# Two transformer layers on one core: where tiles are turned, and in what order each engine works

## The chip, the core and the metric

One core of a Trainium2 chip runs the kernel. The metric is the device time of one execution in microseconds (us), the median over three runs. A profiled execution gives a trace besides; its times are those of the hardware profiler.

## What is computed

The input x has 16 batches of 256 tokens with 512 features, the context 16 x 256 x 384. Two layers follow each other, each an attention to the context and a feed-forward part, cut here to what matters:

```
x = x + L0_xattn(layernorm(x), ctx)     # 16 heads of 32; Q and K normalised to length 1; layer norm with gamma, beta behind
x = x + L0_ffn(layernorm(x))            # times a 512 x 512 Hadamard matrix, rounded to 4 bits, times ternary weights
x = x + L1_xattn(layernorm(x), ctx)     # 16 heads of 32, scores clipped at 1e4
x = x + L1_ffn(layernorm(x))            # 512 -> 2048 -> 512, ternary W1 and W2, exact gelu
```

A matrix product contracts over the partitions, so its left operand has to stand turned, features on partitions. Every fp32 operand is split into an upper fp16 half and a lower one (what is left), and three fp16 products stand for one fp32 product.

## The kernel before

The program is written engine by engine, with semaphores; no scheduler moves anything. It has two phases.

**Phase A** takes the three first sums batch by batch. Its work is cut into steps ("tasks"), in four streams: 0f (front of layer 0: load, layer norm, turn x and ctx, project q, k, v), 0b (heads of layer 0, output projection, and the Hadamard feed-forward), 1f (front of layer 1, with the maxima of the scores) and 1b (heads of layer 1 and its output projection). In iteration i the streams work on batches i, i-1, i-2 and i-3, so there are 19 iterations: 3 in which the streams start, 13 steady ones (3 to 15) and 3 in which they run out. A fifth stream "w" prepares weights in the first two and the last three. A string of digits (`ORDER`, and `ORDERS` for the special iterations) says from which stream the next task comes. All five engines go through this same sequence, each doing its own part of a task.

A **head** task does several things for different heads: ACT takes exp of head h (L946, PSUM to fp32) and casts head h-1 to the upper fp16 half (L954), GpSimd (POOL in the trace) subtracts to get the lower half of h-1 (L802), TensorE multiplies head h-4 with the values (L1510 to L1512), DVE divides a finished group of four (L1246, L1249). In layer 1 DVE clips the scores first (L1166) and TensorE then adds the shift of the softmax (L1413). Scores of a quad of heads are 24 matmuls (L1488).

**Turning.** Where a tile has to stand turned, TensorE transposes 128 x 128 blocks in fp32 into a bank of PSUM (L1352, `turn`), ACT copies the bank to the upper half (L884, `hi`) and DVE subtracts to the lower half (L1084, `lo`). That is done for ctx (6 blocks a batch), x of layer 0 (8), x of layer 1 (8), the attention output of layer 0 (8) and 1 (8), and the input of the Hadamard product (8). Already turned by DMA from fp16 rows are q and k of layer 0 (L678) and the rounded levels (L682): SP issues transposing DMAs.

```
def turn(u, src, chunks, after=()):
    open_bank(u, *after)
    for c in range(chunks):
        mm = te.transpose(bank(u.bank)[:, c * P:(c + 1) * P], src[:, c * P:(c + 1) * P], ident)
    mm.then_inc(filled[u.bank], 1)
```

SP's queue issues all loads and stores but that of x1: it loads x (L647) for the next batch behind the store of x2 (L701), and works in the order of the tasks too. DVE takes the statistics of x (L1073, L1075), GpSimd four small operations for the reciprocal deviation (L769 to L775), and ACT normalises (L879).

W1 and W2 of the last feed-forward part are made ternary at the end of phase A: ACT sums their absolute values (L864), DVE makes the signs (L1063, L1068), TensorE turns them (L1313, 128 transposes) and ACT copies them out of PSUM (L872, L875).

**Phase B** is that last part, in 8 steps of two batches with 16 blocks each: TensorE multiplies up (L1530, `up`), ACT applies gelu (L1002), DVE casts (L1276), GpSimd or DVE subtracts (L834, L1281), TensorE multiplies down (L1540, `down`). The normalised x of the next step (L1078, written by `norm_b` at blocks 7 to 10) is turned by TensorE in the same way, at blocks 9 to 12 (L1523), with ACT (L995) and DVE (L1269) behind; it is needed by the `up` that runs in block 14.

## Time and profile before

| | |
|---|---|
| median of 3 runs | 1884.29 us (1883.42 to 1885.39) |
| the profiled execution | 1877.33 us, span of its trace 1875.5 us |
| TensorE (PE) busy | 1673.7 us, 89% of the span |
| DVE busy | 1225.7 us, 65% |
| ACT busy | 1027.6 us, 55% |
| GpSimd (POOL) busy | 980.5 us, 52% |
| granted clock of TensorE, mean | 0.961 of full speed |
| DMA | 136.47 MB, 73 GB/s in the mean |

A row of the trace has the engine, the line of the code, the operation, the tile written and the tiles read. A wait is booked to the engine that waited, with what released it. A matmul's own duration is longer than the time that it adds in a row of matmuls, since they are pipelined; the distance of starts tells that.

### The profile page before, as it was taken

To read this page: it belongs to the slowest core of one execution; us is meant where nothing else is said; L and a number is where in the kernel's file an instruction comes from. 1 tells how busy PE (TensorE), PEld (TensorE's weight loads), DVE (VectorE), ACT (ScalarE), POOL (GpSimd) and SP (SyncE) were. 2 spreads that over 40 slices of the span, in tenths; PEclk is the share of its full clock that TensorE was granted. 3 is DMA by queue.
4 is the path that set the end of the run, shared out by engine and by line. 5 is a ranking of instruction groups with operands and counts; after the bars stand their busy time and mean duration, and the time that the engine had idled before them with its cause. 6 is when DMAs were issued, how large, how long until landed. Compare 5 with 4: busy or idle time off the path is not lost. (4 is left out here: it accounts for less than half of the span.)

```text
span 1875.5 us, 44682 instructions
## 1 busy us (share of the span) xinstructions
PE 1673.7 (89%) x18098; PEld 986.8 (53%) x18098; DVE 1225.7 (65%) x2444; ACT 1027.6 (55%) x1905; POOL 980.5 (52%) x1073
## 2 busy tenths in 40 slices
PE   5688898998989999989998999977759999999999
PEld 2445655556555565555565555554534444444444
DVE  4748778787787867878687786857854433344332
ACT  4663867758677586765758667586542222222221
POOL 1553857648576485855758567483353222322221
PEclk9789999999999999999999999988968999999999
DMA  7322231322313123031330313236320110011100
GB/s 225 93 88 59 65 111 24 111 58 66 111 24 111 33 91 111 19 110 25 106 100 24 111 24 111 62 112 206 112 68 19 45 45 12 34 45 46 45 23 23
DMA packets 132379, 136.47 MB, mean 73 GB/s; under 512 B 91464, under 2 KB 95688, under 8 KB 131152
## 3 DMA queue, kind: packets, MB, share of 16 engines
q1 hardware_dynamic: 129872, 125.23, 22.6%
q0 software_dynamic: 2304, 8.39, 1.1%
q8 instruction: 145, 2.38, 0.5%
q14 instruction: 58, 0.48, 0.1%
HBM read 72.77 MB, written 31.46 MB: 56 GB/s over the span
## 5 line engine op out<-in xcount | busy, mean ns | idle before, releaser
L802 POOL TENSOR_TENSOR arena<-arena 128x512 f16<-128x512 f32 x512 | 598.6, 1194 | 123.8 <-ACT arena L954 123.1
L946 ACT ACTIVATE arena<-psum 128x512 f32<-128x512 f32 x512 | 311.0, 614 | 78.2 <-PE psum L1413 68.1
L954 ACT ACTIVATE arena<-arena 128x512 f16<-128x512 f32 x512 | 330.5, 653 | 7.6 <-PE psum L1512 7.3
L1002 ACT ACTIVATE arena<-psum,arena 128x512 f32<-128x512 f32 x128 | 88.1, 688 | 352.1 <-PE psum L1530 352.1
L1332 PE MATMUL psum<-arena 128*128 128x512 f16 x672 | 259.8, 387 | 3.5 <-DVE arena L1084 1.8
L1333 PE MATMUL psum<-arena 128*128 128x512 f16 x672 | 258.4, 385 | 0.0
L1336 PE MATMUL psum<-arena 128*128 128x512 f16 x672 | 257.8, 384 | 0.0
L1510 PE MATMUL psum<-arena 128*128 128x33 f16 x2048 | 199.3, 180 | 62.2 <-POOL arena L802 57.3
L834 POOL TENSOR_TENSOR arena<-arena 128x512 f16<-128x512 f32 x64 | 77.3, 1208 | 333.9 <-DVE arena L1276 333.9
L1530 PE MATMUL psum<-arena 128*128 128x512 f16 x1024 | 243.1, 381 | 1.4 <-DVE arena L1269 1.4
L1540 PE MATMUL psum<-arena 128*128 128x512 f16 x1016 | 240.0, 379 | 0.9 <-POOL arena L834 0.9
L1276 DVE CAST arena<-arena 128x512 f16<-128x512 f32 x128 | 54.6, 427 | 272.1 <-ACT arena L1002 272.1
L1510 PEld LDWEIGHTS psum<-arena 128*128 128x128 f16 x2048 | 167.8, 97 | 116.7 <-POOL arena L802 54.1
L814 POOL TENSOR_TENSOR arena<-arena 128x512 f32<-128x512 f32 x32 | 40.0, 1269 | 311.4 <-DVE arena L1220 311.4
L1512 PE MATMUL psum<-arena 128*128 128x33 f16 x2048 | 195.9, 178 | 0.0
L1511 PE MATMUL psum<-arena 128*128 128x32 f16 x2048 | 195.8, 178 | 0.0
L1488 PE MATMUL psum<-arena 32*128 32x256 f16 x4608 | 166.0, 276 | 14.1 <-DVE arena L1128 5.1
L1166 DVE TENSOR_SCALAR psum<-psum 128x512 f32<-128x512 f32 x256 | 158.9, 690 | 29.1 <-PE psum L1488 29.1
L1511 PEld LDWEIGHTS psum<-arena 128*128 128x128 f16 x2048 | 165.3, 97 | 16.3 <-issue 0.3
L1530 PEld LDWEIGHTS psum<-arena 128*128 128x128 f16 x1024 | 100.4, 98 | 123.5 <-issue 1.9
L1512 PEld LDWEIGHTS psum<-arena 128*128 128x128 f16 x2048 | 163.6, 96 | 0.0
L1540 PEld LDWEIGHTS psum<-arena 128*128 128x128 f16 x1016 | 99.2, 98 | 115.0 <-POOL arena L834 1.9
(129 smaller groups left out, 3155.9 us busy)
## 6 DMA issues: line engine op xcount, KB each, us to landing
arena<-in_x SPq DMA_DIRECT2D x32, 512.0 KB, 4.7
arena<-x_scratch SPq DMA_DIRECT2D x32, 512.0 KB, 5.2
arena<-in_L_ffn_W SPq DMA_DIRECT2D x16, 1024.0 KB, 5.4
arena<-arena SPq DMA_DIRECT2D x16, 512.0 KB, 6.5
x_scratch<-arena POOLq DMA_DIRECT2D x16, 512.0 KB, 5.7
x_scratch<-arena SPq DMA_DIRECT2D x16, 512.0 KB, 3.0
out<-arena SPq DMA_DIRECT2D x14, 512.0 KB, 3.5
arena<-in_ctx SPq DMA_DIRECT2D x16, 384.0 KB, 5.2
```

The costliest lines, as they stand in the source:

```text
L802: gp.tensor_tensor(pl[l][:, h % NP, :], pf[l][:, h % NF, :], ph[l][:, h % NP, :], ALU.subtract).then_inc(p_lo[l].sem, 1)
L946: sc.activation(pf[l][:, h % NF, :], bank(u.bank), ACT.Exp, scale=SCALE / (QS * QS) if l == 0 else SCALE).then_inc(read[u.bank], 1)
L954: sc.activation(ph[l][:, h % NP, :], pf[l][:, h % NF, :], ACT.Copy).then_inc(p_hi[l].sem, 1)
L1332: te.matmul(out, x_hi, w[:, 0, c, :], start=(c == 0), stop=False)
L1333: te.matmul(out, x_hi, w[:, 1, c, :], start=False, stop=False)
L1336: mm = te.matmul(out, x_lo, w[:, 0, c, :], start=False, stop=(c == chunks - 1))
L1488: mm = te.matmul(bank(u.bank)[:, k * S:(k + 1) * S], parts[own][rows_g, j, m, k * P:(k + 1) * P], parts[other][rows_g, 1 - j, m, :], start ...
L1510: te.matmul(out, p_hi_t, vs[l][:, k, h, 0:OW], start=(k == 0), stop=False)
L1511: te.matmul(out[:, 0:HD], p_hi_t, vs[l][:, k, h, HD + 2:VP], start=False, stop=False)
L1512: mm = te.matmul(out, p_lo_t, vs[l][:, k, h, 0:OW], start=False, stop=(k == NT - 1))
L1530: mm = te.matmul(bank(4 + f % 2), w1T[:, c, f * P:(f + 1) * P], xTb[slot][:, part, c, :], start=(c + part == 0), stop=(c + part == DC))
L1540: mm = te.matmul(bank(k), src[:, f % NG, k * P:(k + 1) * P], w2T[:, f, :], start=(f + n == 0), stop=(f + n == FC))
```

## The change

1. **Turned by DMA.** For layer 0's x, both attention outputs and the Hadamard input the tile is no longer transposed by TensorE. ACT copies the rows to an fp16 upper half, DVE subtracts to the lower half (both inputs now in SBUF), both halves stand side by side in one row of 1024, and a transposing DMA on SP puts them where the products read them (`turn_rows`). Layer 1's x is still turned by TensorE. The same is done for the normalised x in phase B (`upper_b`, `lower_b`, `turn_b`).
2. **ctx, W1 and W2** are handed over turned. One ACT copy and one DVE subtraction of 128 x 768 per batch make the halves of ctx; the signs of W1 and W2 are written where they are used.
3. **Orders.** `ORDER` and `ORDERS` give every engine its own sequence of the same tasks. TensorE's sequence decides which bank a task gets.
4. In phase B's first step the statistics of x no longer stand behind the last output of phase A.

The core of the diff:

```diff
+def turn_rows(dst, rows, k):
+    return sp.dma_start_transpose(dst.rearrange("p s c n -> p (s c) n")[:, :, k * P:(k + 1) * P],
+                                  rows[:, k].rearrange("p s n -> p (s n)"))
...
 # SP
+elif kind == "split_x" and l == 0:
+    sp.wait_ge(xT_lo.sem, xT_lo.at(b, k + 1))
+    if b > 2:
+        sp.wait_ge(qk_hi.sem, qk_hi.at(b - 3))
+    turn_rows(xT[0], x_rows, k).then_inc(xT_turned[k].sem, 16)
+elif kind == "split_out":
+    sp.wait_ge(oT_lo[l].sem, oT_lo[l].at(b, k + 1))
+    if l == 1 and b + 2 < B:
+        sp.wait_ge(absmax.sem, absmax.at(b + 2, k + 1))
+    turn_rows(oT[l], out_rows[l], k).then_inc(oT_turned[l][k].sem, 16)
+elif kind == "split_ffn":
+    sp.wait_ge(xF_lo.sem, xF_lo.at(b, k + 1))
+    turn_rows(oT[0], out_rows[0], k).then_inc(xF_turned[k].sem, 16)
...
 # ACT
 elif kind == "turn_out":
-    hi(use["ot", l, at[0]], cols(oT[l], 0, at[0]), oT_hi[l].sem)
+    last = use["o", l, H // HG - 1]
+    act.wait_ge(read[last.bank], last.read_at)
+    sc.activation(out_rows[l][:, k, 0, :], attn[l][:, k, :], ACT.Copy).then_inc(oT_hi[l].sem, 1)
...
 # DVE
 elif kind == "split_out":
-    lo(use["ot", l, k], cols(oT[l], 1, k), cols(oT[l], 0, k), oT_hi[l].sem, oT_hi[l].at(b, k + 1))
+    dve.wait_ge(oT_hi[l].sem, oT_hi[l].at(b, k + 1))
+    v.tensor_tensor(out_rows[l][:, k, 1, :], attn[l][:, k, :], out_rows[l][:, k, 0, :],
+                    ALU.subtract).then_inc(oT_lo[l].sem, 1)
 elif kind == "split_ctx":
-    lo(use["c", 0, k], cols(cT[0], 1, k), cols(cT[0], 0, k), ctxT_hi.sem, ctxT_hi.at(b, k + 1))
+    dve.wait_ge(ctxT_hi.sem, ctxT_hi.at(b))
+    v.tensor_tensor(cT[0][:, 1], CT, cT[0][:, 0], ALU.subtract).then_inc(ctxT_lo.sem, 1)
...
 # TensorE
-elif kind == "turn_out":
-    turn(use["ot", l, k], attn[l][:, k, :], DC, [use["o", l, g] for g in range(H // HG)] if k == 0 else [])
 elif kind == "out_project":
-    open_bank(u, use["ot", l, k])
+    open_bank(u)
+    pe.wait_ge(oT_turned[l][k].sem, oT_turned[l][k].at(b))
...
 # orders: one of the tables
+    "steady": {
+        "SP": ("0210000000011111111111111111111111111111100000000031111111111110000000003333333333333333333333333333"
...
 # phase B, TensorE
-        if has_next and 0 <= f - TURN_AT < BT:
-            turn_b(s + 1, f - TURN_AT)
...
-                pe.wait_ge(xTb_read, s * BT + 2 * BT)
+                pe.wait_ge(xTb_turned, 16 * BT * (s + 2))
...
 # host
+arrays["in_ctx_768"] = np.ascontiguousarray(inputs["ctx_768"].transpose(0, 2, 1))
+for name in ("L1_ffn_W1", "L1_ffn_W2"):
+    arrays[f"in_{name}"] = np.ascontiguousarray(inputs[name].T)
```

How the orders move the work, at three places of a steady iteration. First TensorE where an iteration begins: x8 is the ternary product of the batch before, x48 two quads of scores of layer 0. Before:

```order
L1456 MATMUL psum<-arena 128x512 x8
L1405 MATMUL psum<-arena 128x128 x2
L1488 MATMUL psum<-arena 128x256 x48
L1342 MATMUL psum<-arena 128x256
L1344 MATMUL psum<-arena 128x256
L1345 MATMUL psum<-arena 128x256
```

and with the change (L1557 is the old L1456, L1509 the old L1405, L1587 the old L1488, L1609 to L1611 the old L1510 to L1512):

```order
L1557 MATMUL psum<-arena 128x512 x8
L1509 MATMUL psum<-arena 128x128 x2
L1587 MATMUL psum<-arena 128x256 x48
L1609 MATMUL psum<-arena 128x33
L1610 MATMUL psum<-arena 128x32
L1611 MATMUL psum<-arena 128x33
```

Behind the scores stood the projection of layer 1's keys (L1342 to L1346, 40 narrow matmuls); now the first heads' products with the values stand there.

Second DVE at the same point: the last output of layer 1 (L1182, now L1298), maxima (L1154, now L1268), the shifts (L1160, now L1274), the ternary output (L1220, now L1338), then the statistics of the next x. Before:

```order
L1182 SCALAR_TENSOR_TENSOR arena<-psum,arena 128x512
L1154 TENSOR_REDUCE arena<-psum 128x2 x4
L1160 TENSOR_SCALAR arena<-arena 128x2x2x4
L1128 SCALAR_TENSOR_TENSOR arena<-psum,arena 128x16x32
L1220 SCALAR_TENSOR_TENSOR arena<-psum,arena 128x512 x2
L1073 BN_STATS arena<-arena 128x6
```

and with the change:

```order
L1268 TENSOR_REDUCE arena<-psum 128x2 x6
L1298 SCALAR_TENSOR_TENSOR arena<-psum,arena 128x512
L1274 TENSOR_SCALAR arena<-arena 128x2x2x4
L1338 SCALAR_TENSOR_TENSOR arena<-psum,arena 128x512 x2
L1179 BN_STATS arena<-arena 128x6
L1181 BN_AGGR arena<-arena 128x2
```

Four maxima and the values' lower half (L1128) no longer stand between the last output and the statistics.

Third SP over one iteration, from the store of x2 on (L701, now L808; the load of x is L647, now L736). Before:

```order
L701 DMA x_scratch<-arena 128x1024
L653 DMA arena<-ctx_scratch 128x768
L647 DMA arena<-in_x 128x2x512
L648 DMA arena<-in_ctx 128x2x384
L633 DMA arena<-in_x 128x2x512
L635 DMA arena<-arena 128x1024
L640 DMA arena<-x_scratch 128x1024
L685 DMA ctx_scratch<-arena 128x768
L678 DMA_TRANSPOSE arena<-arena 128x8x128 x4
L682 DMA_TRANSPOSE arena<-arena 128x4x128 x2
```

and with the change:

```order
L808 DMA x_scratch<-arena 128x1024
L736 DMA arena<-in_x 128x2x512
L737 DMA arena<-in_ctx 128x3x256
L742 DMA arena<-ctx_scratch 128x768
L722 DMA arena<-in_x 128x2x512
L724 DMA arena<-arena 128x1024
L790 DMA ctx_scratch<-arena 128x768
L713 DMA_TRANSPOSE arena<-arena 128x8x128 x4
L767 DMA_TRANSPOSE arena<-arena 128x8x128 x2
L729 DMA arena<-x_scratch 128x1024
L713 DMA_TRANSPOSE arena<-arena 128x8x128 x2
L767 DMA_TRANSPOSE arena<-arena 128x8x128 x2
L713 DMA_TRANSPOSE arena<-arena 128x8x128 x2
L787 DMA_TRANSPOSE arena<-arena 128x4x128 x2
```

Eight transposing DMAs are added (L713 of the change); those of q and k (L678, now L767) stand between them.

## Rows read from the trace of the kernel before

**Rows 1.** Windows of the steady part, the drain and phase B: busy us and count of each engine, clock, DMA share.
```profile
174.00:1214.00 1040.00, 952.95 (x12868) 606.41 (x12870) 807.23 (x1681) 708.94 (x1383) 677.56 (x754) 0.99 0.26 73
1214.00:1412.00 198.00, 139.22 (x1949) 94.50 (x1942) 139.06 (x236) 120.01 (x202) 107.36 (x97) 0.81 0.38 128
1412.00:1875.50 463.50, 456.92 (x2163) 213.67 (x2162) 171.68 (x338) 104.01 (x159) 120.16 (x107) 0.99 0.09 32
```

**Rows 2.** Timeline of SP: a store of x2, the load of x behind it, the last store.
```profile
415.04 0.32 SPq L701 DMA_DIRECT2D x_scratch<-arena  x1
...
415.88 0.78 SPq L647 DMA_DIRECT2D arena<-in_x  x1
...
1210.13 0.32 SPq L701 DMA_DIRECT2D x_scratch<-arena  x1
```

**Rows 3.** Waits of TensorE, steady iterations (174 to 1214 us).
```profile
PE psum L1413 <- DVE psum L1166: 33.6, 26, 2.3
PE psum L1510 <- POOL arena L802: 31.1, 64, 1.6
```

**Rows 4.** Groups of TensorE: fp32 transposes in the steady stage, and in phase B.
```profile
L1352 PE MATMUL psum<-arena 128*128 128x128 f32 x598 | 90.9, 285 | 11.6 <-DVE arena L1249 9.0 <-DVE arena L1147 1.2
...
L1523 PE MATMUL psum<-arena 128*128 128x128 f32 x128 | 20.7, 292 | 6.4 <-DVE arena L1078 4.5 <-DVE arena L1269 1.9
```

**Rows 5.** Timeline of TensorE at the start of an iteration: start us, duration us.
```profile
497.29 1.79 PE L1488 MATMUL psum<-arena 32*128 32x256 f16 x48
499.01 0.28 PE L1342 MATMUL psum<-arena 128*128 128x256 f16 x1
...
500.11 0.27 PE L1342 MATMUL psum<-arena 128*128 128x256 f16 x1
...
504.29 0.18 PE L1510 MATMUL psum<-arena 128*128 128x33 f16 x1 [0.74 <-POOL arena L802]
...
504.59 1.29 PE L1352 MATMUL psum<-arena 128*128 128x128 f32 x10
...
507.56 0.19 PE L1510 MATMUL psum<-arena 128*128 128x33 f16 x1 [0.60 <-POOL arena L802]
```

**Rows 6.** Timeline of TensorE in phase B.
```profile
1625.75 0.60 PE L1523 MATMUL psum<-arena 128*128 128x128 f32 x4
1626.18 1.89 PE L1540 MATMUL psum<-arena 128*128 128x512 f16 x8
```

**Rows 7.** Line 678 (turned rows of q and k), and the loads of x.
```profile
L678 SPq DMA_TRANSPOSE arena<-arena x64: 1231/1242/3616, 29.3 to 1195.5; - x64
...
DMA to landing us min/median/max: 3.0/3.2/6.0
...
DMA to landing us min/median/max: 3.7/4.7/6.8
```

**Rows 8.** Groups of DVE in the steady stage, by shape.
```profile
L1084 DVE TENSOR_TENSOR arena<-psum,arena 128x512 f16<-128x512 f32 x130 | 86.9, 685 | 33.3 <-ACT arena L884 32.1
...
L1139 DVE SCALAR_TENSOR_TENSOR arena<-arena 128x512 f16<-128x512 f32 x52 | 53.0, 1060 | 0.0
```

**Rows 9.** Timelines of ACT and of GpSimd in the heads of layer 0.
```profile
588.95 0.64 ACT L946 ACTIVATE arena<-psum 128x512 f32<-128x512 f32 x1
...
589.95 0.65 ACT L946 ACTIVATE arena<-psum 128x512 f32<-128x512 f32 x1
...
581.53 0.18 POOL L769 TENSOR_TENSOR arena<-arena 128x2 f32<-128x2 f32 x1 [0.38 <-DVE arena L1075]
...
583.01 4.52 POOL L802 TENSOR_TENSOR arena<-arena 128x512 f16<-128x512 f32 x4
```

**Rows 10.** Timeline between phase A and phase B.
```profile
1402.10 0.68 DVE L1073 BATCH_NORM_STATS2 arena<-arena 128x6 f32<-128x512 f32 x1
...
1402.95 0.66 DVE L1073 BATCH_NORM_STATS2 arena<-arena 128x6 f32<-128x512 f32 x1
...
1414.04 4.98 PE L1530 MATMUL psum<-arena 128*128 128x512 f16 x16 [1.42 <-DVE arena L1269]
```

More of the change, by code:

```diff
@@ L50 @@
 BT = GB * NT
-STATS_AT, NORM_AT, TURN_AT = 3, 7, 9
+STATS_AT, NORM_AT = 3, 7
 class Signal:
@@ L223, in back @@
     return out
+ENGINES = ("SP", "POOL", "ACT", "DVE", "PE")
 POOLS = {"all": tuple(range(8))}
@@ L243, with task_order @@
 PART.update({task: "w" for stream in PREPARE.values() for task in stream})
-TASKS = merged(STREAMS, ORDER)
-def task_order(i):
+def task_order(i, engine):
     active = [0 <= i - n < B for n in range(len(ALL))]
     streams = [stream if x else [] for stream, x in zip(STREAMS, active)] + [PREPARE.get(i, [])]
-    order = ORDERS[i] if i in ORDERS else [n for n in ORDER if active[int(n)]]
+    order = ORDERS.get(i, ORDERS["steady"])[engine]
     return [(PART[task], task) for task in merged(streams, order)]
@@ L717, in _ @@
             for s in range(B // GB - 1):
+                for k in range(BT):
+                    turn_b(s + 1, 1 - s % 2, k)
                 store(s, s % 2)
@@ L1251, in attn_out @@
                         ins.then_inc(read[u.bank], 1)
-            steps(step)
+            steps(step, "DVE")
             def add_b(s, slot):
@@ L1513, in attend @@
                 mm.then_inc(av_done[l].sem, 1)
[L1515 removed]
+            for n, value in enumerate(steps(step, "PE")):
                 pe.wait_ge(read[n], value)
[L1519 to L1524 removed]
             def up(s, slot, f):
```

305 lines of the change are left out of this document (184 added, 121 removed).

## The prediction

> **What bounds the kernel now.** I read four views, coarse to fine. First the stages: the table of windows [rows 1] cuts the span behind a ramp of 174 us into the steady iterations, the drain and phase B. In the steady part TensorE is busy 952.95 of 1040 us, DVE 807, ACT 709, GpSimd 678; in phase B TensorE is busy 456.92 of 463.5 us. Then the beat: ten iterations lie between the first and the last row of [rows 2], (1210.13 - 415.04) / 10 = 79.5 us each; 13 are steady. So per iteration TensorE is busy 952.95 / 1040 x 79.5 = 72.8 us and idle 6.7. Then who it waits for [rows 3]: in the 13 iterations 33.6 us for the clips on DVE before the shift matmuls (2.6 each), 31.1 us for GpSimd's lower halves before the attention-value products (2.4 each). The granted clock there is 0.99, the 2.4 GHz level. So the steady part is bound by TensorE at 92%, and the rest is where an order common to all engines leaves it waiting. Phase B has TensorE alone as its bound. The drain (1214 to 1412) has no engine above 71% and is bound by chains.
>
> **Transposes leave TensorE.** In phase A 46 fp32 transposes run per iteration (598 in 13 [rows 4]); layer 1's x keeps 8, so 38 go. Back to back, four take 1626.18 - 1625.75 = 0.43 us [rows 6]; the 285 ns shown for one [rows 4] are pipelined. At 0.108 us that is 4.1 us per iteration: TensorE's need falls from 72.8 to 68.7 us. In phase B seven of eight steps lose 16 transposes each [rows 4]: 7 x 16 x 0.108 = **-12.1 us**. There nothing else covers them, so they count in full: a turned tile is needed two blocks (6.9 us) after DVE's subtraction of the last, and the DMA lands it in 3.2 us.
>
> **What takes their place.** A turned tile of 128 x 1024 fp16 now goes ACT copy, DVE subtraction, then a transposing DMA on SP: 1.24 us to issue, 3.2 us to landing [rows 7]. Before it was 0.43 + 0.6 + 0.68. So each pair of tiles (x of layer 0, out of layer 0, the Hadamard input, out of layer 1) is 3 to 4 us later. In the new order TensorE has other work there (between the subtraction of out and out_project it does four heads and a quad of scores), so I price this at 0 in the steady part and at its full length in ramp and drain. Eight more issues are 10 us of SP's 79.5: no bound. The DMA share is 0.26 [rows 1] with six such issues and the loads; eight more cannot fill it.
>
> **DVE's reads move from PSUM to SBUF.** The subtraction from PSUM takes 685 ns, whatever else runs; DVE's nearest row with both inputs in SBUF, L1139, has a mean of 1060 ns [rows 8]. Nine such operations per iteration: between 0 (if none meets GpSimd) and 9 x 1.13 = 10.2 us (each waits out a whole GpSimd subtraction, 4.52 / 4 [rows 9]). I take L1139's surplus, 9 x 0.37 = 3.3 us, since it is the same engine pair in the same stage. DVE goes from 807.23 / 1040 x 79.5 = 61.7 to 65 us busy: not yet the bound. The Trainium skill (SBUF — State Buffer, "Who interferes with whom") says that DVE with two SBUF inputs and GpSimd's reads exclude each other for a whole instruction. By that rule read at its worst the term is 10.2 us, not 3.3; the trace agrees in kind (L1139 stretches) and not in that size.
>
> **The start of an iteration gets worse.** This is the new wait. In the old order layer 0's first two quads of scores are followed by 40 narrow matmuls (4.3 us) and only then by the first head's product; in the new one the product follows at once. Score quads take 1.72 / 2 = 0.86 us, a projection of 20 narrow ones 2.2 (ten in 1.10), a head's product 0.3 [rows 5]. The first product needs exp, exp and cast on ACT (a pair takes 1.00 us) and 1.13 us on GpSimd [rows 9], so it is ready some 3.5 us after the first scores began, with 1.7 us of work in between: 1.8 us idle where before it was 0.74 [rows 5]. Second: on DVE the new order has the statistics of x right behind the last output and two small steps, and SP may load x only after that output is stored. The load lands 4.7 us after its issue [rows 7], the issue comes 0.84 us after the store [rows 2], then 2 x 0.85 = 1.7 us of statistics [rows 10] and 583.01 - 581.53 = 1.5 us on GpSimd [rows 9], with which it stands in front of the fourth head's subtraction. Seen from the scores, which start some 0.5 us after that output (a shift and a small matmul lie between): 5.5 - 0.5 + 1.7 + 1.5 = 8.2 us, then six heads at 1.13: the ninth product is ready at 15.0 us. TensorE's own work up to it is four quads, nine products, two projections: 3.4 + 2.7 + 4.4 = 10.5 us. So about 4.5 us idle, where the old order shows 0.74 + 0.60 = 1.3 [rows 5]. That is +3.2 us per iteration.
>
> **What the separate orders give back.** In the old order every engine takes the steps in one sequence. In the new one TensorE has half a projection more between a quad's scores and its shift, which I take to cover half of the 2.6 us; later heads come at GpSimd's pace with projections between, which covers perhaps 1.2 of the 2.4. Bounds: nothing and 5.0. I take 2.5. Idle then is 6.7 + 3.2 - 2.5 = 7.4 us, the iteration 68.7 + 7.4 = 76.1 us, 3.4 less: 13 x 3.4 = **-44 us** (from 0.9 less per iteration with nothing given back, -12, to 5.9 with all, -77).
>
> **Ramp, drain, joint.** Ramp (174 us): some 70 transposes less, -8, against three iterations with later tiles and nothing to cover them, +8: **0** (-8 to +8). Drain (198 us): 40 transposes of tiles and 128 of signs go, 168 x 0.108 = 18 us of a TensorE that is idle 59 of the 198, so I count a third, and with it ACT's 16 copies of the signs and DVE's waits for them; DVE's own work on the signs stays. Two chains get 3 us longer, the rest comes from signs no longer standing between attention steps: **-8** (-20 to 0). Joint: in the old order phase B's statistics run behind the last output of phase A, from 1402.10 on, and its first product comes at 1414.04 [rows 10]; now they stand ahead, but SP issues three of the four turned tiles only behind the last store, so 3 x 1.24 + 2.0 us after it, some 1409.5: **-4** (-8 to +3).
>
> Sum: -12 - 44 + 0 - 8 - 4 = **-68 us** on the profiled execution's 1877.3 us, 1809. The median of the runs shown is 7.0 us above that execution (1884.3), so I forecast 1884.3 - 68 = **1816 us**.
>
> **Rivals.**
> 1. The separate orders close nearly all stalls: idle falls to 4 us, the iteration to 72.7. For: every named wait of [rows 3] is one of order, not of capacity, and no other engine is above 82%. Against: the walk above from scores to the ninth product. 13 x 6.8 + 24 = 112 less: 1772 us. Chance 0.24.
> 2. DVE becomes the bound. It would be busy 61.7 + 10.2 = 71.9 us if each of its nine reads waits out a GpSimd instruction, plus 4 us for x: 76, and if 2.5 us of its present 17.8 us of waiting stays, 78.4 us per iteration, 1.1 less. 14 + 24 = 38 less: 1846 us. For: L1139's mean; against: its surplus is 0.37 us, not 1.13. The rule of the Trainium skill named above is this one's mechanism. Chance 0.18.
> 3. Slower: turned tiles come late at TensorE. Place: the four pairs per iteration, each 1.24 + 3.2 = 4.4 us from subtraction to the second landing, behind loads on one queue. TensorE saves 4.1 us per iteration, and the other stages 24 / 13 = 1.8; so it decides from 5.9 us exposed per iteration, 1.5 per pair. With half of each exposed, 8.8: 13 x 2.9 = 38 more: 1922 us. For: SP takes all in one order; against: TensorE's order has other work behind each pair, and no row of [rows 3] waits for a transposing DMA though six run per iteration. Chance 0.05.
>
> **Numbers.** The forecast 0.51, rivals 0.24, 0.18, 0.05, and 0.02 for a change that nets nothing. A measurement of this kernel tells about 0.2% (4 us) from no change. The range goes from rival 1 to just past rival 2: 1770 to 1852. Faster 0.93, same 0.02, slower 0.05.
>
> **What would show it.** Right: steady beat near 76 us; the attention product's wait for GpSimd above 31 us in total at the start of each iteration, the shift's wait for clips below 33.6; DVE waiting some 4 us per iteration for x; the new subtractions with a mean near 1.05 us; phase B some 12 us shorter from first to last product. Wrong: a beat under 74 or over 78, TensorE waiting on turned tiles by more than 1 us per iteration, or a phase B that is not 12 us shorter.

## The result: slower, and the profile after

The changed kernel takes 1931.4 us in the median (1928.0 to 1937.9, four runs), the kernel before on the same chip 1883.9 (1880.2 to 1885.4): a ratio of 1.026, 95% interval 1.023 to 1.029. The forecast was 1816 us with a range to 1852, so sign and size are both wrong. The profiled execution took 1931.8 us, its span is 1929.3.

The windows of the changed kernel, stage by stage as in [rows 1]: ramp, steady part, drain, phase B.
```profile
core 0: us, PE busy (x) PEld busy (x) DVE busy (x) ACT busy (x) POOL busy (x), PEclk, DMA share, GB/s
0.00:194.00 194.00, 121.88 (x1079) 65.17 (x1079) 112.86 (x193) 95.83 (x163) 83.97 (x116) 0.82 0.48 123
194.00:1272.00 1078.00, 922.52 (x12326) 563.14 (x12327) 877.45 (x1658) 716.05 (x1367) 700.47 (x754) 0.95 0.40 95
1272.00:1474.00 202.00, 131.56 (x1783) 82.12 (x1781) 147.43 (x244) 105.83 (x187) 110.40 (x97) 0.76 0.46 139
1474.00:1929.30 455.30, 445.29 (x2048) 200.80 (x2048) 177.11 (x336) 103.80 (x157) 125.49 (x106) 0.99 0.19 53
```
Against [rows 1] the ramp is 20 us longer, the steady part 38, the drain 4, and phase B 8.2 shorter (where one stage ends and the next begins is placed by eye). TensorE is busy 30 us less in the steady part, DVE 70 us more. The beat, from the timeline of SP with the stores that answer to [rows 2]:
```profile
445.56 0.33 SPq L808 DMA_DIRECT2D x_scratch<-arena  x1
...
1274.75 0.33 SPq L808 DMA_DIRECT2D x_scratch<-arena  x1
```
These are the third and the thirteenth store of x2: (1274.75 - 445.56) / 10 = 82.9 us per iteration, where [rows 2] give 79.5 and the forecast 76.1. From the last store on, the kernel before runs 473.2 us (1402.26 to 1875.5), the changed one 457.3 (1471.97 to 1929.3).

TensorE's waits in the 13 steady iterations of the changed kernel (us in total, times, longest), to be held against [rows 3]:
```profile
PE psum L1609 <- POOL arena L911: 63.9, 58, 3.3
PE psum L1587 <- DVE arena L1268: 26.0, 27, 1.6
PE psum L1609 <- DVE arena L1237: 24.6, 13, 1.9
...
PE psum L1436 <- DVE arena L1261: 7.2, 22, 0.6
PE psum L1547 <- DMA arena<-arena: 4.9, 6, 1.6
PE psum L1436 <- DMA arena<-arena: 4.9, 8, 1.1
```
The shift's wait for the clips is gone, as the new order promised; the wait for GpSimd has doubled, and three waits for DVE are new (L1268 reads the maxima, L1237 the projections of q and k, L1261 the turned projections). The waits for turned tiles are small: 9.8 us in all, 0.8 per iteration. DVE's own waits there, and its groups of instructions by shape (count, busy us, mean ns):
```profile
DVE arena L1227 <- ACT arena L1012: 56.4, 13, 7.3
DVE arena L1179 <- DMA arena<-in_x: 53.3, 13, 5.1
```
```profile
L1253 DVE SCALAR_TENSOR_TENSOR arena<-arena 128x512 f16<-128x512 f32 x52 | 79.6, 1569 | 0.0
...
L1288 DVE TENSOR_TENSOR arena<-arena 128x512 f16<-128x512 f32 x52 | 43.2, 851 | 0.7
...
L1319 DVE TENSOR_TENSOR arena<-arena 128x512 f16<-128x512 f32 x26 | 33.4, 1285 | 14.0 <-ACT arena L1074 13.5
L1224 DVE TENSOR_TENSOR arena<-arena 128x512 f16<-128x512 f32 x26 | 33.0, 1269 | 6.5 <-ACT arena L1007 6.5
...
L1227 DVE TENSOR_TENSOR arena<-arena 128x768 f16<-128x768 f32 x13 | 23.8, 1833 | 56.4 <-ACT arena L1012 56.4
```
The first row is the L1139 of [rows 8], which the change doesn't touch: its mean went from 1060 to 1569 ns. The others are the new subtractions. DVE waits 4.1 us per iteration for x, and 4.3 for ACT's copy of ctx. One iteration in four quarters, before and after:
```profile
493.57:513.61 20.04, 18.57 (x251) 12.77 (x250) 11.09 (x22) 16.37 (x33) 14.48 (x16) 1.00 0.63 218
513.61:533.64 20.03, 17.68 (x284) 11.14 (x283) 14.89 (x33) 18.73 (x39) 18.24 (x19) 1.00 0.18 28
533.64:553.68 20.04, 17.74 (x245) 12.37 (x242) 17.12 (x34) 12.60 (x25) 16.04 (x23) 0.91 0.01 2
553.68:573.71 20.03, 19.39 (x220) 10.32 (x217) 17.64 (x41) 6.63 (x12) 2.98 (x3) 1.00 0.25 41
```
```profile
529.85:550.46 20.61, 15.78 (x258) 11.54 (x257) 11.22 (x22) 18.02 (x35) 17.65 (x19) 0.83 0.72 211
550.46:571.07 20.61, 18.54 (x265) 10.72 (x263) 17.50 (x33) 18.20 (x38) 19.14 (x19) 0.92 0.19 37
571.07:591.68 20.61, 19.56 (x223) 12.33 (x222) 18.38 (x33) 13.71 (x25) 15.48 (x22) 1.00 0.31 66
591.68:612.29 20.61, 17.89 (x207) 9.13 (x205) 20.30 (x44) 5.16 (x9) 1.51 (x1) 1.00 0.37 69
```
This is what an average hides. DVE is busy 81% of the new iteration; it is nearly half idle in the first quarter (11.22 of 20.61 us, about as much as before), 89% busy in the third and full in the last (20.30). Of TensorE's waits for DVE in this iteration 2.3 us stand in the last quarter, 1.9 in the second and 1.0 in the two others. The granted clock (third column from the end; 1.00 is the 2.4 GHz level, 0.50 the 1.2 GHz level) has a mean of 0.83 and 0.92 in the first half, behind TensorE's idle time there.

### The profile page after: what moved, and what is told of

Its sections match the earlier page's. It is cut to its first block and busy times, and to the rows that moved or that the text cites. A ratio compares the mean times of both kernels' runs of the same rounds, so it can differ in the third digit from the quotient of the medians.

```text
span 1929.3 us, 42960 instructions
## 1 busy us (share of the span) xinstructions
PE 1621.3 (84%) x17234; PEld 911.2 (47%) x17234; DVE 1314.9 (68%) x2428; ACT 1021.5 (53%) x1873; POOL 1020.3 (53%) x1073
## 3 DMA queue, kind: packets, MB, share of 16 engines
q1 hardware_dynamic: 300880, 167.19, 34.7%
## 5 line engine op out<-in xcount | busy, mean ns | idle before, releaser
L911 POOL TENSOR_TENSOR arena<-arena 128x512 f16<-128x512 f32 x512 | 636.4, 1267 | 103.1 <-ACT arena L1065 102.2
L1065 ACT ACTIVATE arena<-arena 128x512 f16<-128x512 f32 x512 | 326.4, 641 | 30.7 <-PE psum L1611 29.1
L1057 ACT ACTIVATE arena<-psum 128x512 f32<-128x512 f32 x512 | 307.4, 604 | 55.4 <-PE psum L1517 33.6
L1436 PE MATMUL psum<-arena 128*128 128x512 f16 x672 | 264.1, 393 | 51.7 <-DMA arena<-arena 44.5
L1609 PE MATMUL psum<-arena 128*128 128x33 f16 x2048 | 194.8, 182 | 127.8 <-POOL arena L911 97.6
L1437 PE MATMUL psum<-arena 128*128 128x512 f16 x672 | 263.3, 392 | 0.0
L1440 PE MATMUL psum<-arena 128*128 128x512 f16 x672 | 261.8, 390 | 0.0
L943 POOL TENSOR_TENSOR arena<-arena 128x512 f16<-128x512 f32 x64 | 79.8, 1247 | 325.5 <-DVE arena L1391 325.5
L1622 PE MATMUL psum<-arena 128*128 128x512 f16 x1024 | 244.5, 382 | 7.6 <-DMA arena<-arena 7.6
L1609 PEld LDWEIGHTS psum<-arena 128*128 128x128 f16 x2048 | 166.1, 98 | 177.6 <-issue 65.9
L1632 PE MATMUL psum<-arena 128*128 128x512 f16 x1016 | 240.0, 379 | 1.0 <-POOL arena L943 1.0
L1587 PE MATMUL psum<-arena 32*128 32x256 f16 x4608 | 172.5, 283 | 49.3 <-DVE arena L1268 28.9
L1611 PE MATMUL psum<-arena 128*128 128x33 f16 x2048 | 191.1, 180 | 0.0
L1610 PE MATMUL psum<-arena 128*128 128x32 f16 x2048 | 191.0, 179 | 0.0
L1610 PEld LDWEIGHTS psum<-arena 128*128 128x128 f16 x2048 | 166.2, 98 | 8.2 <-issue 0.6
L1611 PEld LDWEIGHTS psum<-arena 128*128 128x128 f16 x2048 | 164.3, 98 | 0.0
L1622 PEld LDWEIGHTS psum<-arena 128*128 128x128 f16 x1024 | 100.8, 98 | 130.8 <-issue 11.7
L1268 DVE TENSOR_REDUCE arena<-psum 128x2 f32<-128x512 f32 x256 | 157.0, 680 | 0.6 <-PE psum L1587 0.3
```

The costliest lines, as they stand in the source:

```text
L911: gp.tensor_tensor(pl[l][:, h % NP, :], pf[l][:, h % NF, :], ph[l][:, h % NP, :], ALU.subtract).then_inc(p_lo[l].sem, 1)
L1057: sc.activation(pf[l][:, h % NF, :], bank(u.bank), ACT.Exp, scale=SCALE / (QS * QS) if l == 0 else SCALE).then_inc(read[u.bank], 1)
L1065: sc.activation(ph[l][:, h % NP, :], pf[l][:, h % NF, :], ACT.Copy).then_inc(p_hi[l].sem, 1)
L1436: te.matmul(out, x_hi, w[:, 0, c, :], start=(c == 0), stop=False)
L1437: te.matmul(out, x_hi, w[:, 1, c, :], start=False, stop=False)
L1440: mm = te.matmul(out, x_lo, w[:, 0, c, :], start=False, stop=(c == chunks - 1))
```

## The experiments

Four theories, by the letters that the expectations use. **A**: the separate orders cost the time, by the idle stretch at an iteration's start. **B**: DVE costs it, since its subtractions now read two tiles in SBUF and GpSimd's reads hold them up. **C**: turned tiles come late. **D**: with less work and more idle time TensorE falls to its lower clock more often. The beat is always from the third to the thirteenth store of x2, DVE's busy time from the window between the two, each from the run's one profile. The ratio is to the kernel before as it ran beside the run in question (medians 1882.1 to 1883.9). e4, e8, e11 and e15 leave lower halves out of the products, so they compute something less exact and serve only to price work.

| run | median us | ratio to before (interval) | beat | DVE busy |
|---|---|---|---|---|
| before | 1883.9 | 1 | 79.5 | 61.4 |
| changed | 1931.4 | 1.026 (1.023 to 1.029) | 82.9 | 67.2 |
| e1 common order, DMA turning | 2134.6 | 1.135 (1.132 to 1.138) | 95.7 | 65.1 |
| e2 layouts, TensorE turning | 1911.3 | 1.015 (1.014 to 1.017) | 81.9 | 61.9 |
| e3 separate orders, TensorE turning | 2113.5 | 1.124 (1.121 to 1.127) | 97.0 | 62.0 |
| e4 lower halves multiplied by 0 | 1912.4 | 1.016 (1.012 to 1.020) | 81.5 | 64.5 |
| e5 e2 with fillers | 1896.3 | 1.007 (1.004 to 1.011) | 80.8 | 61.8 |
| e6 start filled | 1931.8 | 1.027 (1.024 to 1.030) | 82.7 | 67.5 |
| e7 keys early | 2003.0 | 1.064 (1.060 to 1.068) | 89.1 | 65.8 |
| e8 DVE's lower halves zeroed | 1886.3 | 1.002 (1.001 to 1.004) | 79.8 | 60.1 |
| e9 x2 stored by GpSimd | 1926.7 | 1.023 (1.020 to 1.026) | 83.0 | 67.3 |
| e10 phase B's part alone | 1868.7 | 0.993 (0.991 to 0.995) | 79.6 | 61.4 |
| e11 GpSimd reads nothing | 1866.4 | 0.992 (0.990 to 0.994) | 80.1 | 60.2 |
| e12 e10 and x2 stored by GpSimd | 1848.1 | 0.982 (0.980 to 0.984) | 78.5 | 61.5 |
| e13 e9 and the front early | 1939.6 | 1.032 (1.029 to 1.036) | 83.6 | 66.3 |
| e14 weights' loads early | 1932.3 | 1.027 (1.024 to 1.029) | 83.2 | 67.1 |
| e15 e8 and e11 together | 1839.8 | 0.977 (0.976 to 0.979) | 78.0 | 56.1 |
| e16 before, x2 stored by GpSimd | 1867.5 | 0.992 (0.991 to 0.994) | 78.5 | 61.5 |
| e17 e5's banks alone | 1898.8 | 1.008 (1.006 to 1.010) | 81.6 | 61.6 |

**Orders and turning, each with the other's partner.** e1 gives all engines one order in every iteration, that of the kernel before with ctx's turning taken out:
```
-    "steady": {"SP": ..., "POOL": ..., "ACT": ..., "DVE": ..., "PE": ...},
+    "steady": dict.fromkeys(ENGINES, ("20011131111222102000100110101011010110110333330112000331301113313102103333012031323122333113333331"
...
```


> The changed kernel with all its DMA turning and layouts, but with the one common order of the kernel before for all five engines (the steps that no longer exist taken out). Theory A (the separate orders cost the time, by the idle stretch at an iteration's start and DVE's full end): the beat returns to 76 to 79 us and the time to 1835 to 1875 us. Theory B (the nine subtractions that now read two SBUF inputs, and what they do to their neighbours, cost it, whatever the order): the beat stays near 82.8, the time 1915 to 1940. Theory C (turned tiles late, since the common order has little work between a subtraction and its product): the beat goes to 84 or more, TensorE waits for the transposing DMA by several us per iteration, 1950 or more.

e3 puts the change's five steady orders into the kernel before:
```
-    order = ORDERS[i] if i in ORDERS else [n for n in ORDER if active[int(n)]]
+    order = ORDERS[i] if i in ORDERS else STEADY[engine] if all(active) else [n for n in ORDER if active[int(n)]]
```

> The kernel before, every turn made by TensorE, but its steady iterations in the separate orders of the change (ctx turned ahead of the fifth head on TensorE, and three more steps moved where the added use of banks asks for it). Theory A: the loss comes with the orders alone: beat 82 to 85, time 1915 to 1960. Theory B: without the SBUF subtractions the separate orders are harmless or a gain: beat 77 to 79.5, time 1850 to 1885. Theory C: as B.

Both are far worse than either original: beats of 95.7 and 97.0. e1 came out as C said, with TensorE waiting for turned tiles, in ten iterations:
```profile
PE psum L1375 <- DMA arena<-arena: 76.7, 30, 4.2
...
PE psum L1486 <- DMA arena<-arena: 32.9, 10, 4.1
```
That is 11.0 us per iteration for turned tiles, where the change's own orders leave 0.8. So late tiles (rival 3) are a true price of turning by DMA under the common order, and the separate orders take nearly all of it away. A in the form "the common order is better here" falls. e3 lies outside every range that was given. Its orders had to be adapted (ctx is turned early again), and its largest waits come with that: in ten iterations TensorE's transposes wait 42.4 us for attention outputs on DVE and 35.6 us for the load of ctx. It says that these orders don't suit a kernel that turns on TensorE, and prices nothing in the changed one.

**What DVE's work costs.** e4 replaces the subtractions, here that of x:
```
-  v.tensor_tensor(x_rows[:, k, 1, :], xn[0][:, k, :], x_rows[:, k, 0, :], ALU.subtract)
+  v.tensor_scalar(x_rows[:, k, 1, :], x_rows[:, k, 0, :], 0.0, None, ALU.mult)
```


> The changed kernel, separate orders and all DMAs kept; the eight subtractions per iteration that form the lower halves of x, the attention outputs and the Hadamard input are replaced by a one-input multiplication by 0 of the upper half, so these lower halves are left out of the products (same tiles, same DMAs). Theory B: DVE is rid of about 9 us per iteration and of the mutual exclusion with GpSimd: the beat falls to 75 to 78 and the time to 1830 to 1870. Theory A: DVE is only full because of where things stand; the beat falls by 1 us or less per iteration, time 1912 to 1932. Theory C: unchanged, within 5 us of 1931.

The relief was smaller than expected, 2.7 us of DVE per iteration, since the multiplications still take 731 to 951 ns; the beat fell by 1.4. e8 reads nothing in that place:
```
-  v.tensor_tensor(x_rows[:, k, 1, :], xn[0][:, k, :], x_rows[:, k, 0, :], ALU.subtract)
+  v.memset(x_rows[:, k, 1, :], 0.0)
```

> The changed kernel with its eight subtractions per iteration (lower halves of x, attention outputs, Hadamard input) replaced by filling the same tiles with zeros, which reads nothing; these lower halves are left out of the products. The run before, with a multiplication in their place, took only 2.7 us of DVE's time per iteration away (731 to 951 ns each stayed) and the beat fell by 1.5. Theory B: with some 6 to 8 us less on DVE the beat falls to 78 to 79.5, time 1875 to 1895. Theory A: DVE's relief stops paying, beat 80.5 to 81.5, time 1900 to 1915.

The beat fell from 82.9 to 79.8 (0.3 above B's range, the time inside it), and TensorE's waits tell why. In ten iterations:
```profile
PE psum L1607 <- POOL arena L911: 51.7, 45, 3.1
PE psum L1585 <- DVE arena L1268: 10.2, 10, 1.0
...
PE psum L1607 <- DVE arena L1237: 5.1, 10, 0.5
```
All its waits for DVE come to 19.0 us there, against 49.2 in ten iterations of the changed kernel: 3.0 us less per iteration, and the beat is 3.1 less. The wait for GpSimd is unchanged (51.7 against 49.9), and those for turned tiles didn't shrink (9.8 against 7.0), so it isn't through earlier tiles that e8 gains.

e11 leaves DVE alone and changes GpSimd:
```
-  gp.tensor_tensor(pl[l][:, h % NP, :], pf[l][:, h % NF, :], ph[l][:, h % NP, :], ALU.subtract)
+  gp.memset(pl[l][:, h % NP, :], 0.0)
```


> The changed kernel with GpSimd's 32 subtractions per iteration (lower halves of the attention weights) replaced by filling the same tiles with zeros, which reads nothing; these lower halves are left out of the products. Theory B (DVE's instructions with two SBUF inputs are held by GpSimd's reads): the unit subtraction on DVE falls from a mean of 1569 ns to 650 to 800, the new ones from 850 to 1290 to the same, DVE's busy time per iteration from 67.2 to 56 to 59 us, and the beat to 74 to 78 us. Against B: the means stay over 1000 ns and DVE's busy time over 64 us.

DVE's groups there, in ten iterations:
```profile
L1287 DVE TENSOR_TENSOR arena<-arena 128x512 f16<-128x512 f32 x40 | 38.9, 993 | 0.5
...
L1252 DVE SCALAR_TENSOR_TENSOR arena<-arena 128x512 f16<-128x512 f32 x40 | 28.2, 746 | 0.0
...
L1223 DVE TENSOR_TENSOR arena<-arena 128x512 f16<-128x512 f32 x20 | 13.8, 692 | 13.7 <-ACT arena L1006 13.7
...
L1226 DVE TENSOR_TENSOR arena<-arena 128x768 f16<-128x768 f32 x10 | 9.6, 958 | 40.3 <-ACT arena L1011 40.3
```
The unit subtraction takes 746 ns instead of 1569, that of x 692 instead of 1269, that of ctx 958 instead of 1833: the same instructions, with GpSimd's heads writing and not reading. Undisturbed, x's subtraction costs what the one from PSUM did (685 ns [rows 8]). Only the attention output's (L1287) didn't gain; its mean went from 851 to 993 ns. Three in four take 0.69 us, two of them with GpSimd idle and one beside its filling, and each fourth takes 1.9: it starts while a sum on GpSimd that still reads SBUF (L901) runs, and ends 0.56 us behind it.
```profile
455.62 2.37 POOL L901 TENSOR_TENSOR arena<-arena 128x1024 f32<-128x1024 f32 x1
...
456.63 1.92 DVE L1287 TENSOR_TENSOR arena<-arena 128x512 f16<-128x512 f32 x1
```
The Trainium skill (SBUF — State Buffer, "Who interferes with whom") says that a DVE instruction with two SBUF inputs contends with a GpSimd instruction that reads SBUF, and not with one that only writes it. The run agrees with both halves of that sentence. B's beat of 74 to 78 was not reached (80.1), nor its 56 to 59 us for DVE (60.2). And e11 alone doesn't price DVE: per iteration TensorE's waits for DVE fall from 4.9 to 1.6 us, but those for the attention weights' lower halves fall too, from 5.0 to 2.4, while waits for the load of ctx (1.9) and for turned tiles (2.2) come up. e15 has both reliefs:

> The changed kernel with both reliefs of DVE together: the eight lower-half subtractions on DVE and the 32 on GpSimd replaced by filling the tiles with zeros (these lower halves are left out). Theory B in full (DVE sets the beat, the orders are good once it is free): DVE busy 53 to 57 us per iteration and the beat 75 to 77.5, the forecast's 76.1 reached, time 1815 to 1845. Theory A (the order's own idle stretches hold the beat from some 79.5 on): both together give little more than either, beat 78.5 to 80, time 1855 to 1885.

Two pairs of runs differ in DVE's eight subtractions alone. From the changed kernel to e8 DVE's busy time goes from 67.2 to 60.1 us and the beat from 82.9 to 79.8; from e11 to e15 it goes from 60.2 to 56.1 and the beat from 80.1 to 78.0: 0.44 and 0.5 us of beat per us of DVE. e15's time is in B's range, its beat 0.5 above it. The beat still falls at 56 us, so DVE is not a bound that is reached at some value; it is on the path for part of each iteration. The forecast's 76.1 is missed by 1.9 even so.

**The clock.** e6 puts filler products before TensorE's waits for the first heads:
```
+  for _ in range({0: 26, 1: 4, 2: 4, 3: 4, 4: 4}.get(h, 0) if l == 0 and b > 0 else 0):
+      te.matmul(bank(u.bank)[:, 272:512], identh, wsplit[0, "q"][:, 0, 0, 0:240], start=True, stop=True)
   pe.wait_ge(p_lo[l].sem, p_lo[l].at(b, h + 1))
```


> The changed kernel with filler products (240 columns into the unused part of the output bank) ahead of TensorE's waits for the first five heads of layer 0: 26 ahead of the first, 4 ahead of each of the next four; they fill its idle stretch at an iteration's start, nothing reads them. Theory D: the clock stays at 2.4 GHz there, the beat falls by 1 to 3 us (two of three falls gone), time 1890 to 1918. Theory A (the order alone: the waits are GpSimd's and DVE's, and only the time lost waiting counts): no gain, the fillers cost up to 1 us: 1930 to 1945. Theory B (DVE is the engine that sets the beat): within 5 us of 1931.

The windows at an iteration's start, of the changed kernel and of e6:
```profile
529.85:535.00 5.15, 2.20 (x52) 1.30 (x50) 1.32 (x3) 4.16 (x9) 4.08 (x4) 1.00 0.80 254
535.00:540.15 5.15, 3.70 (x48) 2.84 (x49) 1.64 (x4) 5.08 (x10) 4.92 (x9) 0.55 1.04 359
540.15:545.31 5.16, 5.16 (x75) 4.16 (x73) 3.53 (x3) 3.62 (x7) 4.68 (x4) 0.79 0.33 129
```
```profile
529.06:534.14 5.08, 4.78 (x78) 3.76 (x76) 1.31 (x3) 4.10 (x9) 4.02 (x4) 1.00 0.83 259
534.14:539.22 5.08, 4.52 (x67) 3.55 (x66) 1.64 (x4) 5.01 (x10) 4.84 (x9) 1.00 1.01 359
539.22:544.30 5.08, 5.08 (x101) 4.50 (x99) 3.63 (x3) 3.71 (x8) 4.88 (x4) 1.00 0.35 133
```
TensorE was busy 2.20 of 5.15 us, and then ran at 0.55 and 0.79 of full speed; with the fillers the clock stays at 1.00. The time doesn't move (1931.8 against 1931.4), as A and B had it. D is not the cause of the loss. In e6 TensorE's own work takes some 68.9 us of the iteration instead of 71.0, and waits and fillers together 13.8 instead of 11.9: what the faster clock gives goes into waiting.

**The order at an iteration's start.** e7 moves TensorE's key projections of layer 1:
```
- scores 0, scores 1, product 0, product 1, product 2, keys 0, product 3, scores 2, product 4, keys 1
+ scores 0, scores 1, keys 0, product 0, product 1, product 2, keys 1, product 3, scores 2, product 4
```


> The changed kernel with one change in TensorE's steady order: the two turned projections of layer 1's keys stand ahead of the first and the fourth head's product instead of behind the third and the fifth, so real work covers the idle stretch at an iteration's start. Theory A with the clock: up to 3 us of idle and up to 3 us of slow clock go, part of it given back where the projections stood: beat 79 to 81.5, time 1890 to 1915. Theory B: DVE sets the beat, within 6 us of 1931.

Both theories missed: 6.2 us per iteration more. TensorE now waits for the load of ctx that these projections need, and for DVE, in ten iterations:
```profile
PE psum L1447 <- DMA arena<-ctx_scratch: 54.0, 10, 7.2
PE psum L1610 <- DVE arena L1262: 40.3, 20, 4.1
```
e9 takes the store of x2 from SP, in front of whose next load it stands, and gives it to GpSimd:
```
-  sp.dma_start(batch(x2d, b), X[1]).then_inc(x2_stored.sem, 16)
+  pool.dma_start(batch(x2d, b), X[1]).then_inc(x2_stored.sem, 16)
```


> The changed kernel with the store of layer 1's output issued by GpSimd instead of SP, so that SP's load of the next x no longer stands behind it. Theory A+B (DVE, 67.2 of 82.8 us busy, is what the iteration goes round on, and its wait for x, 4.1 us per iteration, is lost at full price): the wait falls below 1 us and the beat to 79 to 80.5 us, time 1885 to 1905. Rival (DVE's wait for x only takes the place of a later one, for the copy of ctx on ACT, 4.1 us per iteration): that wait grows, the beat stays within 1 us of 82.8, time 1918 to 1935.

The rival holds. DVE's wait for x is gone and its wait for ctx has grown by as much:
```profile
DVE arena L1227 <- ACT arena L1012: 86.6, 10, 8.9
```
e13 then moves what that wait is for, on ACT, and x's reciprocal deviation on GpSimd likewise:
```
  ACT
- head 4, head 5, head 6, head 7, normalise x, split ctx, turn x 0
+ head 4, normalise x, split ctx, turn x 0, head 5, head 6, head 7
  GpSimd
- head 1, head 2, head 3, stats x
+ head 1, stats x, head 2, head 3
```

> The changed kernel with layer 1's output stored by GpSimd (DVE's wait then moved from x to ctx, 8.7 us per iteration) and, in ACT's and GpSimd's steady orders, the front of the next batch ahead: on GpSimd the reciprocal root of x ahead of the third head instead of behind the fourth, on ACT the normalising of x and the copy of ctx ahead of the sixth head instead of behind the eighth. Theory (order at the start): DVE's wait for ctx falls from 8.7 to 4 to 6 us and the beat from 82.9 to 79 to 81, time 1885 to 1910. Rival (ACT's heads feed TensorE, so what DVE gains TensorE loses waiting for the later heads): beat 82 to 84, time 1920 to 1945.

Again the rival: DVE's wait for ctx fell from 8.7 to 6.4 us per iteration, one for ACT's turned projections (4.4) came up, TensorE waited 1.4 us more for GpSimd's lower halves than in e9, and the beat went to 83.6. None of the three moves tried here frees the start.

**The ramp.** e14 changes SP's order in iteration 0:
```
- split ctx, store ctx, ..., split x 0, weight 0, weight 1, split x 1, ..., turn unit 0, ..., turn unit 1, weight 2, weight 3
+ weight 0, weight 1, ..., split ctx, store ctx, ..., split x 0, split x 1, ..., weight 2, turn unit 0, ..., weight 3, turn unit 1
```


> The changed kernel with SP's order of the first iteration alone changed: the loads of the third and fourth weights stand ahead of the turned tiles of x, those of layer 1's k and q (issued at 50.2 and 50.8 us in the changed kernel, at 24.7 and 36.3 before) ahead of the turned unit rows. Theory (the ramp's 20 us come from loads queued behind transposing DMAs on SP): the first store of layer 1's output comes 8 to 16 us earlier than at 281.0, time 1915 to 1923. Rival (the ramp is longer because turned tiles themselves come late at TensorE, whatever the loads): 0 to 3 us, time 1928 to 1935.

The loads went out at 37.1 and 44.5 us instead of 50.2 and 50.8, and the first store of x2 came at 280.7 instead of 281.0 us. So the ramp doesn't turn on where these two loads stand in SP's queue. In e11 that store comes at 264.7 and in e15 at 263.6, in e8 at 277.4: of the ramp's loss, 23 us by that store (257.6 before), 16 go when GpSimd stops reading. Whether through DVE's reads or through the earlier lower halves, these runs don't tell.

**Parts of the change alone.** e2 keeps the layouts and phase B's turning, and turns the rest on TensorE in the common order. e5 adds fillers to it, and e17 has `range(1)` for their `range(CC)`:
```
+  elif kind == "split_ctx":
+      for n in range(NT):
+          u = use["pad", 0, n]
+          open_bank(u)
+          for c in range(CC):
+              mm = te.transpose(bank(u.bank)[:, c % 4 * P:(c % 4 + 1) * P], ident, ident)
+          mm.then_inc(read[u.bank], 1)
```

> The common order of the kernel before; in phase A x, the attention outputs and the Hadamard input are turned by TensorE as before; kept of the change are only the layouts of ctx, W1 and W2 and the DMA turning in phase B. All theories: 12 transposes less per iteration are 1.3 us of TensorE, phase B 8 us shorter as in the changed kernel, the drain without the turning of the signs: beat 78 to 79, time 1845 to 1872. Above 1884 would mean that the loss is in these parts, which none of A, B and C says.

> The layouts-only kernel of the run before (81.9 us per iteration, two falls of the granted clock in each) with 12 filler transposes of a constant put back where TensorE turned ctx; nothing reads them, the result is the same. Theory D (TensorE with less to do falls to its lower clock once more per iteration, and that costs more than the transposes did): the second fall goes, the beat returns to 79 to 80 us, time 1875 to 1890. Theory of order (the loss of the layouts-only kernel is in the single copy and subtraction of ctx on ACT and DVE and in the changed use of banks, not in the clock): more work on TensorE and nothing gained, beat 82 to 83.5, time 1911 to 1930.

> The layouts-only kernel with the two bank uses of the filler run but one filler transpose in each instead of six: the same banks for every product as with the fillers, and 10 transposes (1.1 us) less on TensorE. If the rotation of the banks gained the 1.1 us: beat 79.7 to 80.9, time 1882 to 1897, the two bank waits gone. If the clock did: the beat is 81.5 to 82, time 1905 to 1912.

All expected e2 to gain; it lost 2.4 us per iteration. The expectations count the transposes wrongly: the traces show 400 in ten iterations of e2 and 460 before, so 6 less per iteration and not 12, and 6 fillers in e5 and 2 in e17. Its clock is 0.96 in the steady part against 0.99, and TensorE has two new waits, in ten iterations:
```profile
PE psum L1552 <- DVE arena L1296: 9.8, 10, 1.0
PE psum L1552 <- DVE arena L1144: 9.4, 9, 1.1
```
A quad of scores waits for banks there: the plan deals the eight banks out in the order of uses, and without ctx's uses each later product gets another bank. With the fillers these two waits are gone, the clock is 0.98, and the time 15 us less. e17 has nearly e5's median (1898.8, but 1888 to 1907) at e2's clock (0.96), and from the first to the last store of x2 the profiles give 1167.8 us for e5, 1169.8 for e17 and 1180.9 for e2: that speaks for the banks. Its beat between the third and the thirteenth store, 81.6, speaks for the clock. This stays open, and so do the 1.3 us per iteration by which e5 is still above the kernel before. What is shown is that six useless transposes with their two uses of banks gained 15 us.

The changed kernel deals out its banks without ctx's uses too. Its scores wait 18.6 us in ten iterations for a bank that DVE's maxima still read (L1268), and some 10 us of that are left in e8 and in e15. No run gives it other banks, so this rival, 1 to 2 us per iteration by that row, stands untested.

e10 goes back from e2 to ctx as before, and takes the change's orders for the last iteration:
```
+    out += [("turn_ctx", 0, k) for k in ks] + [("split_ctx", 0, k) for k in ks] + [("store_ctx", 0)]
-    out += [("split_ctx", 0), ("store_ctx", 0)]
```


> Phase A as in the kernel before in its one common order, ctx turned by TensorE too; kept of the change are W1 and W2 laid out turned, phase B's DMA turning, and the change's separate orders for the last iteration of the drain alone. Expected by all theories, since nothing in the steady iterations differs: beat 79.4, drain 185 to 192, from the last store to the end 457 to 460 as in the changed kernel (before: 473): 1858 to 1872. If the beat is 81 or more, a change of banks or places in phase A costs it, which none of the theories says.

Time and end came out as expected: 1868.7 us, from the last store to the end 458.7. The drain didn't get shorter, though: 194.2 us from the thirteenth to the last store, 192.1 before. e2 points to the orders of the last iteration for this end: with the common order the transposing DMAs of phase B's first tiles start 9.3 us behind the last store and its first product 17.3 us behind it, where e10 and the changed kernel have 6.8. e16 and e12 add the edit of e9, the store by GpSimd, to the kernel before and to e10:

> The kernel before, with nothing changed but the store of layer 1's output, issued by GpSimd instead of SP. If the gain of the run with both parts (1868.7 to 1848.1) belongs to this store: 1858 to 1868 here, beat 78.3 to 78.8. If it needed phase B's part: 1878 to 1884.

> The run before last (phase B's part alone) with the store of layer 1's output issued by GpSimd too. DVE waits for x only 1.4 us per iteration in the kernel before, and TensorE is the bound there: theory of the bound: at most 0.5 us per iteration, time from 10 us less to 3 more than that run. Rival: GpSimd's issue and slower landing delay its first lower halves of an iteration, TensorE waits for them: up to 1 us per iteration more, 15 us slower.

e16 gains 15.1 us against the kernel before beside it, 1.0 per iteration (79.5 to 78.5), as expected. DVE's wait for x (14.0 us in ten iterations) is nearly gone (0.6), and TensorE's wait for GpSimd fell from 24.4 to 16.7. e12 missed its range for the better: 1.0 us per iteration and not 0.5 at most. With 1848.1 us, 1.8% less than before, it is the fastest run that leaves nothing out. It gains 34.7 us where the two parts alone gain 14.2 and 15.1; the 5 us more are found behind the last store (453.7 us to the end instead of e10's 458.7), since phase B's turned tiles stood behind that store on SP as well.

## Why the prediction was wrong

**Phase B and the joint: right.** -12 and -4 were forecast, 15.9 us were saved from the last store on: the first product comes 6.8 us after it instead of 11.8 (-5.0; [rows 10] and the rows below), and from there to the end it is 10.9 us less. One slip is in the working: 1409.5 is 7.2 us behind the last store, and 3 x 1.24 + 2.0 gives 5.7.
```profile
1470.78 0.38 PE L1440 MATMUL psum<-arena 128*128 128x512 f16 x1
1478.76 6.37 PE L1622 MATMUL psum<-arena 128*128 128x512 f16 x16 [7.60 <-DMA arena<-arena]
```
**TensorE's need: right.** 68.7 us per iteration were forecast. In e6, at a clock of 0.99, it is busy 73.5. The first 26 of its 42 fillers take 2.84 us, so all of them some 4.6; the rest is 68.9. In the changed kernel itself, at a clock of 0.95, it is 71.0.

**The start of the iteration: right in TensorE's idle time, incomplete on DVE.** Forecast: 4.5 us idle up to the ninth product, DVE waiting 4 us for x. The timelines of TensorE, then of DVE and ACT:
```profile
530.38 0.84 PE L1587 MATMUL psum<-arena 32*128 32x256 f16 x24
531.43 0.84 PE L1587 MATMUL psum<-arena 32*128 32x256 f16 x24 [0.21 <-DVE arena L1338]
535.32 0.18 PE L1609 MATMUL psum<-arena 128*128 128x33 f16 x1 [3.06 <-POOL arena L911]
...
536.35 0.21 PE L1609 MATMUL psum<-arena 128*128 128x33 f16 x1 [0.54 <-POOL arena L911]
...
537.46 0.21 PE L1609 MATMUL psum<-arena 128*128 128x33 f16 x1 [0.58 <-POOL arena L911]
```
```profile
612.21 1.40 DVE L1338 SCALAR_TENSOR_TENSOR arena<-psum,arena 128x512 f32<-128x512 f32 x2
617.97 0.69 DVE L1179 BATCH_NORM_STATS2 arena<-arena 128x6 f32<-128x512 f32 x1 [4.36 <-DMA arena<-in_x]
```
```profile
622.83 0.83 ACT L1012 ACTIVATE arena<-arena 128x768 f16<-128x768 f32 x1
```
TensorE's idle time is 0.21 + 3.06 + 0.54 + 0.58 = 4.4 us and DVE's wait for x 4.1. Not seen: behind the statistics DVE subtracts ctx, whose copy on ACT (622.83) stands behind eight heads. That is 4.3 us more, and the forecast priced both waits only by what they do to TensorE.

**"DVE goes 61.7 to 65 us busy: not yet the bound": the step that failed.** The sum let DVE's added work cost nothing as long as DVE was not full, and counted only TensorE's busy and idle time. The size was off too, but that is the smaller part: DVE went to 67.2. The moved subtractions cost 3.9 us per iteration instead of 3.3 (the 156 instructions of L1084 in 13 iterations came to 7.7 us each iteration; L1190, L1224, L1227, L1288 and L1319 come to 11.6). And L1139's mean, the yardstick, was itself a result of how DVE and GpSimd met: under the new order it stretched by 0.51 us, four times, 2.0 us that no term held. That the size alone doesn't explain it is seen in e4: with DVE at 64.5 us, under the forecast's 65, the beat is 81.5, 5.4 too long. What failed is the use: 65 of 76 was read as room. With 8.4 us of waits at the start and 89 and 98% busy in the last two quarters, DVE had little. TensorE's waits for it (all but the clips) are 26.0 + 24.6 + 7.2 in the rows above, 4.4 us per iteration. Taking DVE's eight subtractions away gives 3.1 us of beat back (e8), and taking the reads of GpSimd's heads away too 4.9, of 6.8 by which the beat was missed; part of the second step is TensorE's shorter wait for GpSimd. The last 1.9 us stay open.

**"The separate orders give back 2.5": half right.** The shift's 2.6 us did go (33.6 us in [rows 3], no such row of TensorE with the change). The waits for DVE that came in its place were not in the sum.

**Turned tiles at 0 in the steady part: right**, 0.8 us per iteration; the row that would have shown the danger is e1's 11.0.

**Ramp at 0 and drain at -8: wrong**, +20 and +4. Late tiles were the only cost that the ramp's bounds (-8 to +8) held; GpSimd's reads, with which 16 us of it go, were not among them. By the windows the steady part was missed by 82 us (38 more instead of 44 less), the ramp by 20, the drain by 12, and phase B with the joint by 8 (8.2 less instead of 16; the rest of its 15.9 falls into the drain's window): 122 us, near the 122.8 from 1809 to 1931.8.

**The rivals.** Rival 2 named the engine and the contention, but not how they cost: it made DVE the one bound, and a us of DVE less gives only 0.44 to 0.5 us. Its DVE total was close by luck (76 with the wait for x; measured 67.2 + 8.4 = 75.6): it had 4.7 us too much of busy time and lacked the wait for ctx. Its beat, 78.4, was 4.5 too short: it let DVE keep only 2.5 us of other waiting and held TensorE's own waits for nothing. The time came out near rival 3's 1922, but not by its mechanism (0.8 us per iteration for turned tiles, where it needed 5.9). Rival 1 and rival 3 are refuted for these orders.

## What to carry to other kernels

In a periodic schedule, compare the engines' busy shares quarter by quarter: an engine at 81% in the mean can be full for a quarter, and here each us added to it was paid by nearly half. A read moved from PSUM to SBUF is priced with its neighbours, since a DVE instruction with two inputs in SBUF is held up wherever it meets a reading GpSimd instruction, and a new order changes where the untouched ones meet them. And take a large change apart: the part in phase B, and one store moved to another queue, gave 1.8% together, while the layout of ctx in the common order lost.

## What was not expected of the hardware

- A multiplication by 0 on DVE with one fp16 input in SBUF took 731 to 951 ns in the mean (e4), no less than the 678 ns of the subtraction that reads PSUM; filling the same tile took 272 ns (e8). The means hide two cases: with GpSimd idle it takes 0.29 us, and one that starts beside GpSimd's sum L901 takes 1.77. The Trainium skill (SBUF — State Buffer, "Who interferes with whom") has single-input operations on DVE contend with GpSimd in some modes; the trace of e4 agrees.
- With eight more transposing DMAs per iteration the load of x lands after 6.0 us in the median instead of 4.7 [rows 7].
- Filling TensorE's idle stretch brought its clock back from 0.55 to 1.00 and no time at all (e6).
